# GNN layer with gathered edges: the record table pre-filled with differing destinations instead of zeros

## What is computed

```
h   = relu(layernorm(x))                       # 12500 x 64
e   = silu([h[src], h[dst], w] @ eW1 + eb1)    # 212500 x 128
e   = silu(e @ eW2 + eb2)
agg = segment_sum(e, src)                      # sums per src node
out = x + silu([h, agg] @ nW1 + nb1) @ nW2 + nb2
```

## Time and profile before

| what | us |
|---|---|
| runs (median; lowest to highest of 3) | 3587.26; 3580.35 to 3598.74 |
| the profiled execution's own time | 3582.76 |
| its span, first to last instruction | 3580.7 |
| TensorE busy, GpSimd busy | 2958.6 (83%), 2506.4 (70%) |
| gather instructions (L406): count, median | 1876, 0.944 |

### The profile page before, as it was taken

One profiled execution on the slowest core, in us unless ns is written; L12 is line 12 of the kernel. 1 busy time (PEld: TensorE's weight loads), 2 busy tenths in 40 slices (PEclk: granted clock), 3 DMA queues, 4 the chain that ended last, 5 costly groups with the idle time before them and its releaser, 6 DMA issues.

```text
span 3580.7 us, 85658 instructions
## 1 busy us (share of the span) xinstructions
PE 2958.6 (83%) x23419; PEld 2453.0 (69%) x23420; DVE 2326.4 (65%) x7772; ACT 1959.8 (55%) x4347; POOL 2506.4 (70%) x2570
## 2 busy tenths in 40 slices
PE   4888888988868888888888888888888888887679
PEld 2567766767767777777777777777777777776554
DVE  8898888788746666666666666666666666665441
ACT  1599999899954444444444444444444444444321
POOL 0288788687777777777777777777777777776530
PEclk7698889798769999999999999999999999999989
DMA  2000010000012222222222222222222222225882
GB/s 83 15 16 24 18 24 18 15 24 18 13 27 54 54 54 54 54 54 54 54 54 54 54 54 53 54 54 54 54 54 54 54 54 54 54 54 47 39 83 51
DMA packets 379589, 161.46 MB, mean 45 GB/s; under 512 B 324822, under 2 KB 347670, under 8 KB 379478
## 3 DMA queue, kind: packets, MB, share of 16 engines
q0 software_dynamic: 75008, 126.93, 16.1%
q1 hardware_dynamic: 304310, 32.32, 7.1%
q10 hardware_dynamic: 160, 0.85, 0.1%
HBM read 139.38 MB, written 20.53 MB: 45 GB/s over the span
## 4 chain that ended last, share of the span: by engine, by line
PE 69%; issue 14%; ACT 10%; DVE 5%; POOL 1%; SPq 1%; DMA 1%; ACTq 0%; DVEq 0%; POOLq 0%
PE bk L907 14%; PE bk L926 13%; PE bk L917 12%; PE bk L905 9%; PE bk L836 6%; ACT BIG L1022 5%; PE bk L895 5%; ACT BIG L1030 3%; PE bk L915 3%; PE bk L823 1%; PE bk L824 1%; PE bk L868 1%; PE bk L859 1%; DVE BIG L482 1%; DVE GA L539 1%
## 5 line engine op out<-in xcount | busy, mean ns | idle before, releaser
L406 POOL DMA_INDIRECT GA<-q_d,RB x1876 | 1793.6, 956 | 625.8 <-issue 486.8
L702 DVE SCALAR_TENSOR_TENSOR GA<-c_bc,RB,GA 128x128 f32<-128x128 f32 x1876 | 616.4, 353 | 572.8 <-DMA GA<-q_d,RB 569.5
L905 PE MATMUL bk<-identf,GA 128*128 128x128 f32 x1876 | 538.3, 287 | 387.4 <-issue 383.5
L1100 ACT ACTIVATE ED<-bk,eb1c 128x512 f32<-128x512 f32 x469 | 322.2, 687 | 906.4 <-PE bk L907 906.4
L712 DVE TENSOR_TENSOR BIG<-bk,BIG 128x128 f32 x1876 | 547.3, 292 | 366.3 <-issue 174.1
L907 PE MATMUL bk<-OHS,P 128*128 128x128 bf16 x5628 | 746.2, 226 | 0.1
L387 POOL DMA_INDIRECT rec_d<-BIG,GA x468 | 530.6, 1134 | 171.8 <-issue 85.3
L836 PEld LDWEIGHTS bk<-BIG 128*128 128x128 f32 x3328 | 512.1, 229 | 171.4 <-issue 120.2
L907 PEld LDWEIGHTS bk<-OHS,P 128*128 x5628 | 541.4, 97 | 115.0 <-issue 0.2
L836 PE MATMUL bk<-BIG 128*128 128x72 f32 x3328 | 520.6, 311 | 77.8 <-ACT BIG L1030 47.1
L905 PEld LDWEIGHTS bk<-identf,GA 128*128 128x128 f32 x1876 | 266.6, 142 | 461.7 <-issue 461.7
(11 more groups left out here) (181 smaller groups left out, 2796.3 us busy)
## 6 DMA issues: line engine op xcount, KB each, us to landing
GA<-q_d,RB POOLq DMA_INDIRECT x1876, 2.5
RB<-rec_d SPq DMA_DIRECT2D x469, 8.0 KB
rec_d<-BIG,GA POOLq DMA_INDIRECT x468
q_d<-QS SPq DMA_DIRECT2D x14, 448.0 KB
rec_d<-ED SPq DMA_DIRECT2D x16, 236.0 KB, 10.8
hT_d<-HT SPq DMA_DIRECT2D x14, 224.0 KB
P<-hT_d SPq DMA_DIRECT2D x8, 384.0 KB, 9.3
P<-in_x SPq DMA_DIRECT2D x8, 384.0 KB, 8.8
```

The source lines that it names most:

```text
L406: e.indirect_dma_start(G[k * U + u], None, q_d, bass.IndirectOffsetOnAxis(ap=RB[k][:, u, 1:2], axis=0))\
L702: ins = e.scalar_tensor_tensor(out=G[k * U + u], in0=c_bc[:, :], scalar=RB[k][:, u, 2:3].bitcast(fp32), in1=G[k * U + u], op0=ALU.mult, op ...
L905: e.matmul(z, G[k * U + u], identf[:, :], is_transpose=True, start=True, stop=False)
L1100: e.activation(E1[k % 2], banks[2 + k % 2][:, :], ACT.Silu, bias=eb1c[:, :]).then_inc(s["e1"], 1)
```

## The change

Word 1 of the records in the fill tile is no longer 0. A new iota on GpSimd writes r + 97 p into word 1 of record r (0 to 117) of partition p (0 to 127), that is 0 to 12,436, each a valid row of `q_d`; SyncE waits for it too. The new instruction stands between L368 and the four iotas of L371. Nothing else is edited; the stores of the fill have the same shape and count.

```
-            e.wait_ge(s["ini"], 1)
+            e.wait_ge(s["ini"], 2)
             init_d = rec_d[0:16 * IR * P // R, :].rearrange("c (r w) -> (c r) w", w=4)
...
             e.memset(INI, 0).then_inc(s["cst"], 1)
             e.wait_ge(s["cst"], 1)
             e.memset(iv.bitcast(fp32)[:, :, 0:1], -1.0).then_inc(s["ini"], 1)
+            e.iota(iv[:, :, 1:2], pattern=[[1, IR], [0, 1]], base=0, channel_multiplier=97).then_inc(s["ini"], 1)
```

## The result

The changed kernel takes 3549.9 us (median of 4; 3541.9 to 3557.0) against 3591.2 us (median of 4) for the kernel before on the same chip: ratio 0.9887, 95% interval 0.9847 to 0.9926. Faster, by 41 us or 1.1%. In a second measurement of the same code, five rounds, it took 3533.1 us (3517.1 to 3550.0) against 3591.1: ratio 0.9859 (0.9836 to 0.9883), which is 51 us; the two medians alone lie 58 us apart.

A forecast was written before the change was run, and what follows sets the result against it. The prediction took GpSimd's gather issue rate to bound the edge loop, with DMA engines limiting the empty tiles' gathers. Savings of 49.7 + 0.4 = 50.1 us from the median 3587.3 gave 3537 us, range 3525 to 3555.

The forecast's parts named there:

- the tail: Gathers of the 112 empty tiles ending the edge loop, said to be engine-limited at 1.71 us each by repeated row 0.
- the step from 1.41 to 1.71 us: Empty tiles' gathers: from the DMA engines' queue time for one gather to the observed pace.
- The rival of a cost by size alone: Empty tiles' gathers: transfer cost depends only on size, slowness on place in the run; no gain, 3587 us, chance 0.05.
- The 112 tiles: Empty tiles at the edge loop's end return to GpSimd's pace, 189.7 to 140.0 us: 49.7 us saved.
- The open price: Engine time for gathering 128 neighbouring rows in an empty tile: between 0.22 and 1.41 us, taken as 0.22.
- half a gain: Empty tiles: neighbouring rows collide too, deciding from 1.19 us of engine time a gather; 3562 us, chance 0.05.
- a loss: Empty tiles: neighbouring rows are worse than one row, deciding from 1.71 us a gather; 3630 us, chance 0.02.
- The loop's end: From the last gather's start to the node stage's first load: 7.07 us before, 0.4 us saved.
- The 6.69 us: Time in a steady group from the last gather to the end of the last L907, read from the earlier trace.
- The rows at blocks' ends: 5,740 never-written rows in blocks' last tiles: landings fall from up to 3.5 to 2.5 us, 0 us saved.
- The rival of a larger gain: Blocks' ends do cost time in the loop's middle, up to 30 us; half of it gives 3522 us, chance 0.03.
- The iota: Added instruction at the start takes 0.18 to 0.9 us, ending before SyncE reaches its wait: 0 us.

The follow-up runs named there:

- the iota of zeros: The changed kernel with its added iota writing 0 everywhere, so all empty rows gather row 0 again; ratio 1.0012 to the kernel before.
- row 6000: The changed kernel with its added iota writing 6000 everywhere, so all empty rows gather that row; 3591.1 us at the usual pace, 4291.8 us on the slow chip.

## Why the prediction was right

**The bound and the cause.** GpSimd's pace bounds the loop, and the common row slows the tail: the iota of zeros (tail 1.687 us) and row 6000 (1.687) against five fills with differing rows (1.252 to 1.270) leave no other reason. Why the engines need longer for it stays open. The prediction said that the tail was limited by the engines, and put the step from 1.41 to 1.71 us on the records and an uneven filling of the queues. The records' queue is 3.8%, the uneven filling is in no view, and the engines stood at 87%, not 100%. What the trace shows is the 13 waits ahead of groups. The rival of a cost by size alone is out: the same 64 KB land after 11.1, 2.8 or 2.5 us. The Trainium skill, "DMA: Bandwidth & Descriptors", section "Bandwidth", gives 0.95 us for 64 KB and doesn't distinguish which rows are read. The traces do: 64 KB from one row hold the engines 1.42 us and land after 10.7, 64 KB from differing rows 0.21 us and 2.4.

**The 112 tiles.** Forecast 49.7 us, measured 48.7 in the first profile and 49.4 in the second (189.7 - 140.3). The open price, that of neighbouring rows, was taken at the lower bound of 0.22 us and measured 0.21 and 0.22; the rivals of half a gain and of a loss needed 1.19 and 1.71.

**The loop's end.** Mis-sized: 0.4 us forecast, 2.4 measured. The 6.69 us came of a wrong reading of the earlier trace rows: the gather at 3205.36 us is not the last of its group but the third, number 1715. The last is number 1716, at 3206.60, and it landed after 3.2 us. The group ahead of it is an ordinary one:

```profile
3201.59 0.96 POOL L406 DMA_INDIRECT GA<-q_d,RB  x1 [0.30 <-PE bk L907]
...
3205.83 0.41 PE L907 MATMUL bk<-OHS,P 128*128 128x128 bf16 x3
...
3206.60 0.94 POOL L406 DMA_INDIRECT GA<-q_d,RB  x1 [0.30 <-DMA RB<-rec_d]
```

From its last gather, number 1712, to the end of the last L907 it takes 3206.24 - 3201.59 = 4.65 us, and 7.07 - 4.65 = 2.4 us is what was measured. On the usual chips the runs with differing rows take 4.66 to 5.07 us, those with one common row 6.9 to 7.4. The difference lies in the landing: from the last gather to its `weigh` it is 4.85 us before and 2.42 after.

**The rows at blocks' ends.** 0 forecast and 0 measured in time, though the landings fell by the 1 us seen in gather 651. The rival of a larger gain needed a faster middle; it was 1.0 us slower in this pair. Over all traces of the usual chips the 1764 gathers take 2221.9 to 2223.6 us with a common row and 2219.7 to 2224.6 with differing ones, so at most a microsecond or two of the 30.

**The iota.** 0 forecast. It took 0.62 us, inside 0.18 to 0.9, and was done 0.45 us ahead of SyncE's wait; nothing is later for it at 119 us. In whole runs a cost of up to 11 us isn't excluded.

**What the sum left out** is that the part ahead of the loop varies by itself: first gathers between 1034.2 and 1065.5 us in ten traces of the usual chips. The runs' spread, from which the range was made, holds this; that the first median lies inside the range, 13 us above the forecast, is owed to that spread and not to a term of the sum. The difference of one profiled pair, 39.8 us, would have been wrong by a fifth as a measure of the change.

## What to carry to other kernels

A gather whose rows are padding still reads: give padding differing indices, at least a handful, since one row asked for by all 128 partitions cost six times the engine time of 128 differing rows. (Two rows were enough here.) Whether that costs anything depends on the pace of what issues the gathers: it showed at 1.26 us a gather and not at 1.66, nor where such gathers stand singly. And the better question behind it is why the empty tiles are computed: 141 us of the 190 are left, and only a loop that ends with the data's last tile would give them back. A count fixed for these inputs (3398.5 us) shows what that is worth, but isn't such a loop.

## What was not expected

- One common row cost 1.37 to 1.47 us of the 16 engines for 128 requests, two rows 0.36, four 0.24 (0.22 and 0.23 on the slow chip), and 128 random ones 0.22 to 0.25. The step between one row and two is not explained by these runs.
- Neighbouring rows (0.22 us) were slightly cheaper than rows 54 KB apart (0.25 us) on the same chip, one profile each.
- One chip ran the kernel before in 4308.1 us, with a wait of 1.9 us once a group ahead of GpSimd's gathers that the trace ascribes to "remote", as it does longer ones of ScalarE and VectorE. The cause stays open. That chip had one run of each kernel.
